# Two joined expert mixtures of a Trainium2 kernel, split into parts of 8, 12, 8 and 4 token groups on both sides

## The reference

```python
# mixture: logits = xn @ gate; the two largest of 8; gates = softmax over these two
#   GELU:   h = gelu(xn @ w1[e] + b1[e]);            y_e = h @ w2[e] + b2[e]
#   SwiGLU: h = silu(xn @ s1[e]) * (xn @ s3[e]);     y_e = h @ s2[e]
#   out  = sum over the two experts of gate_e * y_e
# GELU:   x = x + 0.5 * layernorm(out) * g + 0.5 * b
# SwiGLU: x = x + 0.5 * out
```

## Time and profile before

| | us |
|---|---|
| median of 3 runs | 1300.44 |
| lowest and highest | 1296.27, 1300.60 |
| the profiled execution, its own time | 1300.79 |
| its span, first to last instruction | 1299.0 |
| PE busy in the span | 1008.0 (78%) |
| DVE, ACT, POOL busy | 876.0, 600.8, 770.2 |
| joint program, first to last product (lines 597, 608) | 379.3 to 796.7 |

### The profile page before, as it was taken

How to read it: one execution, slowest core, us unless ns; L and a number is a source line. 1 busy time by engine, 2 the same in 40 slices (tenths; PEclk the granted TensorE clock), 3 DMA queues, 4 the chain that set the end, 5 groups by cost and what they waited for, 6 DMA issues and landing times. The chain is left out here.

```text
span 1299.0 us, 28153 instructions
## 1 busy us (share of the span) xinstructions
PE 1008.0 (78%) x6835; PEld 849.6 (65%) x6836; DVE 876.0 (67%) x3115; ACT 600.8 (46%) x1746; POOL 770.2 (59%) x800
## 2 busy tenths in 40 slices
PE   2599999377465999978788695599889874599892
PEld 2499999344255999968787595244344434589892
DVE  5655678477783566786477464589978967566763
ACT  1266777566233657655344253451345131245562
POOL 2787458720057666785757676176625643777565
PEclk9999999787868999999899798699999995799997
DMA  8644354200012333323233243000000000234353
GB/s 238 223 134 136 100 153 134 64 1 0 1 51 72 99 99 97 96 83 91 85 102 90 94 130 83 8 1 1 1 1 0 0 0 15 91 116 124 102 151 105
DMA packets 146195, 102.93 MB, mean 79 GB/s; under 512 B 16324, under 2 KB 134934, under 8 KB 146070
## 3 DMA queue, kind: packets, MB, share of 16 engines
q1 hardware_dynamic: 70530, 39.35, 10.4%
q0 software_dynamic: 16384, 33.59, 8.7%
q10 hardware_dynamic: 59156, 28.57, 7.5%
HBM read 52.44 MB, written 49.02 MB: 78 GB/s over the span
## 5 line engine op out<-in xcount | busy, mean ns | idle before, releaser
L597 PE MATMUL gelu_hb<-gelu_xsT,gelu_weights 128*128 128x128 f32 x2208 | 303.5, 283 | 2.6 <-issue 2.6
L597 PEld LDWEIGHTS gelu_hb<-gelu_xsT,gelu_weights 128*128 128x128 f32 x2208 | 279.8, 199 | 2.9 <-issue 2.8
L694 ACT ACTIVATE gelu_hid<-gelu_hb,gelu_weights 128x128 f32<-128x128 f32 x736 | 209.7, 374 | 121.5 <-PE gelu_hb L597 90.7
L1237 POOL DMA_INDIRECT slots_x<-gelu_xn,gelu_index x176 | 177.5, 1009 | 92.3 <-DVE gelu_index L936 41.6
L608 PE MATMUL gelu_ob<-w,gelu_hid 128*128 x1472 | 196.7, 277 | 3.6 <-DVE gelu_ys L976 3.4
L608 PEld LDWEIGHTS gelu_ob<-w,gelu_hid 128*128 128x128 f32 x1472 | 181.0, 194 | 4.4 <-issue 4.3
L988 DVE COPY gelu_weights<-w 128x516 f32 x184 | 85.6, 483 | 66.1 <-issue 34.7
L1913 POOL TENSOR_TENSOR rwkv_tw<-rwkv_tw,rwkv_qr 128x512 f32<-128x512 f32 x64 | 79.5, 1273 | 54.3 <-DVE rwkv_tw L1872 45.4
L597 PE MATMUL swiglu_hb<-swiglu_xsT,swiglu_weights 128*128 128x128 f32 x736 | 100.2, 281 | 0.0
L976 DVE TENSOR_TENSOR gelu_ys<-gelu_ob,bias 128x128 f32<-128x128 f32 x184 | 49.9, 289 | 72.5 <-PE gelu_ob L608 70.3
L597 PEld LDWEIGHTS swiglu_hb<-swiglu_xsT,swiglu_weights 128*128 128x128 f32 x736 | 92.3, 197 | 0.0
(11 more groups left out here) (384 smaller groups left out, 2130.3 us busy)
## 6 DMA issues: line engine op xcount, KB each, us to landing
gelu_xs<-slots_x SPq DMA_DIRECT2D x69, 256.0 KB
slots_y<-gelu_ys ACTq DMA_DIRECT2D x138, 128.0 KB
swiglu_xs<-slots_x SPq DMA_DIRECT2D x23, 256.0 KB
slots_y<-swiglu_ys ACTq DMA_DIRECT2D x46, 128.0 KB
raw_s<-in_L_ffn_w ACTq DMA_DIRECT2D x12, 256.0 KB
slots_x<-zeros SPq DMA_DIRECT2D x2, 1472.0 KB, 9.8
slots_x<-gelu_xn,gelu_index POOLq DMA_INDIRECT x176, 2.3
w<-in_L_ffn_w SPq DMA_DIRECT2D x1, 2048.0 KB, 13.7
```

What stands on the lines that cost most here:

```text
L597: last = pe.matmul(hb[j][:, c * P:(c + 1) * P], weights[:, odd * BODY + j, c * P:(c + 1) * P], xsT[j // SET][:, j % SET, :], start=True, s ...
L694: last = act.activation(hid[:, j % RING, c * P:(c + 1) * P], hb[j][:, c * P:(c + 1) * P], ACT.Gelu, bias=weights[:, odd * BODY + j, FF + c ...
L1237: pool.indirect_dma_start(slots_x[:, :], bass.IndirectOffsetOnAxis(index[p][:, k, g:g + 1], 0), tokens[p][:, g, :], None).then_inc(sent[p] ...
```

## The change

The GELU parts of the joint program get 8, 12, 8, 4 groups, like its SwiGLU parts, so that SwiGLU part p needs GELU part p - 4 alone. The parts then begin at tiles 0, 23, 54, 77, 92, 115, 146 and 169. The buffer for the normalised tokens and those for the gathered results are shared between part p and part p + 4, and GpSimd waits on `combined` instead of `sent` before it gathers into them. The hand-made tables are rewritten to match; GpSimd's list from part 0's gathers on is now that of the single mixtures as far as part 3's scatters. No transfer, product or vector operation is added or dropped in number, apart from the pauses that go with the grouping of the transfers.

```diff
-("gelu", "swiglu"): ((4, 12, 8, 8), (8, 12, 8, 4))}
+("gelu", "swiglu"): ((8, 12, 8, 4), (8, 12, 8, 4))}
...
-            tokens += [of(apart, 0, behind), of(xn, GROUP0[2], behind + 1),
-                       of(xn, 0, behind + 2), of(xn, PART_GROUPS[behind + 2], behind + 3)]
+            tokens += tokens
...
-        DRAWER = [0, 1, 2, 3, 1, 2, 1, 3][:NPARTS]
+        DRAWER = [p % PARTS for p in ALL]
...
+            one, other = spare
+            narrow = [t[:, PART_GROUPS[1]:PART_GROUPS[1] + PART_GROUPS[3], :] for t in (other, apart)]
+            back = [halves(one, PART_GROUPS[0]), [of(t, 0, 1) for t in (other, apart)], halves(one, PART_GROUPS[2]), narrow] * 2
...
   PE beside, joint program (iteration: {after tile: work})
+   13: {3: at(turn_tokens, 4, 0)},
+   22: {2: at(turn_tokens, 5, 0), 3: at(turn_tokens, 5, 1)},
+   27: {1: at(turn_tokens, 6, 0) + at(turn_tokens, 6, 1) + at(logits, 6, 0) + at(logits, 6, 1) + at(count_tokens, 6)},
+   29: {3: at(turn_tokens, 7, 0)},
...
   DVE beside, joint program
+   12: {0: at(finish, 0, 0), 1: at(finish, 0, 1), 2: at(stats, 4)},
+   16: {1: at(places, 4)},
+   19: {0: at(finish, 1, 0), 2: at(combine, 1, 2), 3: at(norm, 1, 2)},
+   21: {0: at(finish, 1, 2), 1: at(stats, 5)},
+   22: {0: at(normalise, 5)},
+   24: {0: at(route, 5)},
+   25: {0: at(places, 5)},
+   26: {0: at(table, 5), 2: at(combine, 2, 0), 3: at(norm, 2, 0)},
+   27: {0: at(combine, 2, 1) + at(norm, 2, 1),
+        1: at(finish, 2, 0) + at(finish, 2, 1) + at(combine, 3, 0) + at(norm, 3, 0)
+           + at(stats, 6) + at(normalise, 6) + at(route, 6)},
+   28: {0: at(places, 6), 2: at(finish, 3, 0), 3: at(stats, 7)},
+   29: {0: at(gates, 4), 2: at(normalise, 7)},
...
   POOL's list, joint program
-            send(1, after=(-2, 2) if both else at_tile(0))
+            send(1, after=at_tile(0))
-                fetch(0, q, after=at_tile(27 if both else 29 + 5 * q))
-            send(3, after=at_tile(34 if both else 40))
+                fetch(0, q, after=at_tile(29 + 5 * q))
+            send(3, after=at_tile(40))
...
+                final_power(0, 0)
+                final_power(0, 1)
+                power(4)
             await_sets(-(-TILE0[2] // SET))
+                for q in range(QUADS[1]):
+                    fetch(1, q, after=at_tile(58 + 5 * q))
                 final_power(1, 0)
                 final_power(1, 1)
+                send(4, range(0, 4), after=at_tile(74))
+                final_power(1, 2)
+                send(4, range(4, 8), after=at_tile(79))
+                power(5)
+                gate_power(4)
+                pool.wait_ge(combined, QUAD0[1])
                 await_sets(-(-TILE0[3] // SET))
+                fetch(2, 0, after=at_tile(85))
+                fetch(2, 1, after=at_tile(90, 2))
+                await_sets(TILE0[4] // SET)
+                fetch(3, 0, after=at_tile(96, 2))
+                send(5, range(0, 4), after=at_tile(103, 1))
                 final_power(2, 0)
                 final_power(2, 1)
+                send(5, range(4, 8), after=at_tile(104, 1))
+                final_power(3, 0)
+                power(6)
+                send(5, range(8, 12), after=at_tile(105, 1))
                 gate_power(5)
+                pool.wait_ge(combined, QUAD0[3])
                 await_sets(-(-TILE0[5] // SET))
+                fetch(4, 0, after=at_tile(109, 1))
                 power(7)
+                fetch(4, 1, after=at_tile(114, 2))
+                send(6, after=at_tile(121, 3))
                 gate_power(6)
+                send(7, after=at_tile(134, 3))
```

More of the change, by code:

```diff
@@ L801, in _ @@
[L801 to L806 removed]
+                                           6: {0: at(copy_tokens, 3, 0)},
@@ L1138, in _ @@
-                                           13: {0: at(gates, 3)},
-                                           14: {1: at(finish, 0, 0)},
-                                           15: {1: at(combine, 1, 0) + at(norm, 1, 0), 3: at(finish, 1, 0)},
-                                           16: {0: at(stats, 4), 3: at(normalise, 4)},
-                                           17: {0: at(combine, 1, 1) + at(norm, 1, 1), 3: at(route, 4)},
-                                           18: {0: at(finish, 1, 1), 1: at(places, 4), 3: at(combine, 1, 2) + at(norm, 1, 2)},
@@ L1144, in _ @@
-                                           19: {0: at(table, 4), 2: at(combine, 2, 0) + at(norm, 2, 0)},
-                                           20: {1: at(finish, 1, 2), 2: at(finish, 2, 0), 3: at(stats, 5)},
-                                           21: {0: at(normalise, 5)},
-                                           22: {1: at(route, 5)},
-                                           23: {0: at(places, 5), 2: at(table, 5), 3: at(combine, 2, 1) + at(norm, 2, 1)},
-                                           24: {1: at(gates, 4)},
@@ L1150, in _ @@
-                                           25: {2: at(finish, 2, 1)},
-                                           28: {2: at(gates, 5)},
-                                           29: {0: at(combine, 3, 0) + at(norm, 3, 0)},
-                                           30: {1: at(combine, 3, 1) + at(norm, 3, 1), 3: at(finish, 3, 0)},
-                                           31: {0: at(stats, 6), 1: at(finish, 3, 1), 3: at(normalise, 6)},
-                                           32: {1: at(stats, 7), 3: at(route, 6)},
@@ new lines, in _ @@
+                                           13: {1: at(normalise, 4)},
+                                           14: {0: at(gates, 3)},
+                                           15: {0: at(route, 4)},
+                                           16: {1: at(places, 4)},
+                                           17: {0: at(table, 4), 2: at(combine, 1, 0), 3: at(norm, 1, 0)},
+                                           18: {2: at(combine, 1, 1), 3: at(norm, 1, 1)},
+                                           19: {0: at(finish, 1, 0), 2: at(combine, 1, 2), 3: at(norm, 1, 2)},
@@ L1280, in _ @@
                 power(3)
-            send(2, after=at_tile(15 if both else 18))
+            send(2, after=at_tile(18))
             gate_power(2)
@@ L1299, in _ @@
-                power(4)
-                fetch(1, 2, choices=[0], after=at_tile(67))
                 final_power(1, 1)
-                fetch(1, 2, choices=[1], after=at_tile(69))
-                for p in range(PARTS):
-                    pool.wait_ge(sent[p], SENT[p])
-                await_sets(-(-TILE0[3] // SET))
-                fetch(2, 0, after=at_tile(74))
-                send(4, range(0, 4), after=at_tile(78, 1))
-                final_power(1, 2)
-                final_power(2, 0)
```

114 lines of the change are left out of this document (46 added, 68 removed).

## The result

The changed kernel took 1307.91 us (median of 4 runs, 1307.69 to 1308.93) where the kernel before took 1300.06 on the same chip (4 runs): a ratio of 1.006, 95% interval 1.0038 to 1.0082. The forecast was 1292.9, so the sign was wrong. The time is that of the first rival and the second, almost to the microsecond, but neither is what happened: GpSimd did not wait for part 5's index, and tiles 120 to 143 were not slow behind their first wait. The profiled execution took 1307.69, with a span of 1305.8.

What follows compares the result with a forecast made beforehand. It took the first half as set by how soon part 1 is scattered, the second by GpSimd's list and its waits. Terms +14.9, -19.7, -15.7, +25.2, -11.4, -1.2 gave -7.9 from 1300.8: 1292.9 us, range 1281 to 1309.

Steps and rivals of the forecast that it cites:

- the first rival: VectorE gets slower and is late with part 5's index, GpSimd waits 15.0 us: 1307.9 us; chance 0.22 with all else slower.
- The second rival: Tiles 120 to 143 run at the old 2.46 us each, tile 144 at 742.5: 1307.8 us, half way 1300.4; chance 0.22.
- The start: Ahead of tile 0: a first part of 8 groups instead of 4 costs 14.9 us; tile 0 starts at 394.2.
- Tiles 0 to 55: First 56 tiles: the 12.2 us wait goes, they take the first mixture's 111.7 us; tile 56 4.8 us sooner, at 505.9.
- The store that starts the gathers: Part 1's gathers wait until tile 53 is stored, 4.4 us after tile 56 starts, at 510.3.
- GpSimd's list: From part 1's gathers at 510.3 to the end of part 5's scatters at 647.7, priced from transfers, pauses and powers.
- Part 5's index: VectorE forms it by 603.1, GpSimd comes to the scatters at 610.3: 7.2 us in hand, no wait.
- TensorE idle ahead of tile 112: Iteration 27: TensorE idle some 35 us since GpSimd is late; tile 112 starts at 655.3, 4.7 us later than before.
- The added wait: At tile 120: power(7) stands behind part 4's gathers, which need tiles 114 and 115 stored; a 14 us stall.
- Tiles 120 to 143: Six iterations at 42.1 us plus 2 for restarting at half clock; tile 144 at 727.6, a gain of 6.7 us.
- the third: VectorE and TensorE keep up and GpSimd alone sets the pace, tile 144 at 721.4: 1286.7 us; chance 0.14.
- No slowing by VectorE's copies: Part 4's scatters among GELU tiles priced as elsewhere; the skill page's rule, up to 40 us more, got 0.01 chance.

Runs made afterwards that it cites:

- power(7) first: Changed kernel with power(7) moved ahead of GpSimd's wait for the store, behind gate_power(5): 1305.14 us; 1560.01 us on the slow chip.
- part 6's scatters first: Changed kernel with part 6's scatters and power(7) ahead of GpSimd's store wait, part 4's combines later: 1290.03 us; 1555.80 on the slow chip.
- three kernels here: On part 6's scatters first: gates later, 1290.22 us; that plus part 4's scatters before a final power, 1291.14; part 3's gathers behind part 5's scatters, 1295.89.

## Why the prediction was wrong

Its mechanism held at nearly every stage, and it failed by the size of its terms: four of them behind the first were too small by over a microsecond, and none was too large by more than 0.7 us up to tile 144. It missed by 15.0 us. Up to tile 144 the terms missed by 0.5 (start), 5.4 (tiles 0 to 55), 1.1 (the store that starts the gathers), 6.0 (GpSimd's list), -0.7 (last scatter to tile 112), 4.6 (the added wait) and 0.4 (tiles 120 to 143): 17.3 together. Behind that tile some 2 us came back, in small steps in the joint program and the layers behind it, which no run here explains.

- **The start.** 14.9 us forecast, 15.4 measured. Right.
- **Tiles 0 to 55.** The wait of 12.2 us at tile 12 went. But taking "its 111.7 us for 56 tiles" from the first mixture was the first step to fail: they took 117.2. The bound beside it ("a few us") named the cause, VectorE shared with the first combines, and the value left it out. Of the 5.4 us, iteration 12 has 4.0, and moving two small pieces of VectorE's work gave 3.7 of these back. It gave nothing in the time, so this term's miss was not simply passed on to the end.
- **The store that starts the gathers.** 4.4 us behind tile 56 forecast, 5.5 measured.
- **GpSimd's list**, part 1's gathers to part 5's scatters: 137.4 forecast, 143.4 measured (517.3 to 660.7). The transfers were as priced. The 6.0 are two waits for a variance, 3.3 and 2.7 us. The forecast had priced the powers and not what they wait for.
- **Part 5's index.** 7.2 us in hand forecast, 2.1 found. No wait, so right, but by luck: tile 100 started at 611.6, later than the 603.6 from which the first rival was to decide, and GpSimd did not wait only because it was itself 9.5 us late.
- **TensorE idle ahead of tile 112.** Forecast some 35 us in iteration 27. The iteration lasted 41.4 us where four tiles take 7.6, so it was about 34 us too long; but TensorE was busy for 14.7 us of it, with part 6's turning and logits beside the tiles and a granted clock of 0.59, and idle for 26.7. The length was right, the idle time was not.
- **The added wait.** 14 us forecast, 15.7 measured, at the same tile, from the same queue; the run with power(7) first shows that cause: 25.2 to 10.2 us. But the pause came 8.2 us behind the start of tile 118, not 4.4, so all of it was 3.8 later. The rows say why: VectorE had `finish(3, 0)`, `stats(7)` and `gates(4)` (674.6 to 682.2) ahead of the copy whose store GpSimd waited for. No run moves them.
- **Tiles 120 to 143.** 44.1 us forecast, 44.5 measured. The second rival (59.0) is out, and so is the third, by which tile 144 was to start at 721.4.
- **No slowing by VectorE's copies.** Part 4's 16 scatters, now among GELU tiles, took 0.96 to 1.48 us each (561.4 to 584.0), and the 192 scatters of GELU tokens 1005 ns in the mean. One scatter of part 5 took 2.77 us (at 636.79), and no weight copy ran beside it. Of part 4's 16 scatters, 11 overlap one of VectorE's weight copies (0.43 us each) and took 1.04 us in the mean, the other 5 took 0.97. The Trainium skill, "SBUF — State Buffer", section "SBUF: two separate sides", has such a transfer blocked until VectorE's copy has ended. By that a copy of 0.43 us could hold one back by half a microsecond at most (an estimate from that page and the copies here), and the 40 us of the forecast's estimate were more than the page's rule gives for copies this short. The trace shows 0.07 us in the mean and 0.5 once, so it agrees with a short wait at most.

So the forecast went wrong by adding lengths of work taken from places where nobody was owed anything. Its sum gave 12.5 us less for the tiles from 0 to 55, the start of the gathers and GpSimd's list than they took, and 4.6 less for the added wait; of that, hand-overs to and from VectorE and what the clock made of one of them account for 4.0 (iteration 12), 3.3, 2.7 and 3.8, all of one sign. And the wait of 15 us stood in the forecast as a price of the change. The runs add that it belongs to the list's order and not to the change. Not tried: separate buffers in place of the shared ones, the parts of 8, 12, 8, 4 with the old pairing, and the old parts with a list mended in the same way.

One slip in the recorded text, without effect on its sum: what it calls tile 90's turn, at 578.9, is the transpose of tiles 92 and 93, as 734.82 above is that of tiles 144 and 145.

## What to carry to other kernels

In a list written by hand for one engine, put an instruction that another engine waits for ahead of any wait for a store that comes later; and when a stall goes, the loop comes sooner to everything behind it, so look at what each engine then waits for: here ScalarE and VectorE came too soon for gathers and a power that had not moved, and 3.1 us were got where 7.4 were expected. With part 6's scatters ahead of the wait as well, and the readers of part 4's gathers later, it was 18.2. When a length is taken from another stage, add the small waits of the hand-overs: here they had one sign. Where two engines keep each other at the same pace within about 2 us, relieving the one gained nothing that could be told from zero in three kernels here (tile 112 at 665.8, 668.0 and 667.6 for 667.5); relieving both gained 3 us at that tile.

## Of the hardware

- The same kernel before took 1300.1, 1301.0, 1301.7 and 1550.2 us on four occasions, the last on a chip whose records show 19.3 us of "issue" idle before weight loads of one line where another shows 0.4. What that idle time is, the profile doesn't say. Idle time of that kind makes differences in order hard to read: the kernels with power(7) first and with part 6's scatters first are 15.1 us apart on the one chip (1305.14 and 1290.03), and on the other 4.2 by the medians (1560.01 and 1555.80) and 13 by the ratios on record (1.0107 and 1.0024), with intervals that overlap and single runs 22 us apart. Whether the difference is smaller there is not shown.
- A wait of 2.0 us of TensorE cost 3.7: in that iteration the granted clock fell from 1.00 to a mean of 0.85, and a block of products that takes 1.06 us at 2.4 GHz took 1.92, which is near the lower of the two levels, 1.2 GHz.
